# SBUF laid out with the large tensors first and the small columns last, in a fused attention-and-FFN block

## What is computed

```python
def attn(x):                       # x is layer-normalised already
    n = ln(x, g, b)
    W1, W2 = mlp(n, h1_w1, h1_b1, h1_w2, h1_b2), mlp(n, h2_w1, h2_b1, h2_w2, h2_b2)   # 128 -> 512 -> 128, gelu
    t = tril(W1 @ W2.T) @ n
    x1 = x + ln(gelu(t), g, b)
    return x + mlp(ln(x1, g, b), fm_w1, fm_b1, fm_w2, fm_b2)

def ffn(x):                        # ternary weights, each with a scale by output feature
    h = silu(x @ w1 * s1) * (x @ w2 * s2)          # 128 -> 512
    h = gelu(gelu(h @ a * sa) @ b * sb)            # 512 -> 512 -> 512
    return h @ w3 * s3                             # 512 -> 128

x = x + layernorm(attn(layernorm(x)))
x = x + layernorm(ffn(layernorm(x)))
```

## Time and profile before

| | |
|---|---|
| median of 3 runs | 364.95 us (364.9 to 365.11) |
| profiled execution, its own time | 365.25 us |
| its span, first to last instruction | 363.5 us |
| PE busy in the span | 351.9 us, 97%, 1786 matmuls |
| DVE, ACT, POOL busy | 319.9, 302.2, 153.2 us |
| mean granted TensorE clock | 0.995 |

### The profile page before, as it was taken

One profiled execution on the slowest core, in us unless ns is written; L12 is line 12 of the kernel. 1 busy time (PEld: TensorE's weight loads), 2 busy tenths in 40 slices (PEclk: granted clock), 3 DMA queues, 4 the chain that ended last, 5 costly groups with the idle time before them and its releaser, 6 DMA issues.

```text
span 363.5 us, 6043 instructions
## 1 busy us (share of the span) xinstructions
PE 351.9 (97%) x1786; PEld 290.1 (80%) x1786; DVE 319.9 (88%) x953; ACT 302.2 (83%) x546; POOL 153.2 (42%) x227
## 2 busy tenths in 40 slices
PE   6999999999999999999999999999999999999991
PEld 5886888788888888888888888888788878778990
DVE  5989999999999999899968999998878998958844
ACT  5999999996888979976789798889698489769890
POOL 3587868430581165109430276025450292053311
PEclk9999999999999999999999999999999999999998
DMA  7614300000000000000000000001010001000101
GB/s 231 174 58 148 114 4 1 0 3 0 3 0 0 2 9 23 0 0 2 1 29 3 0 2 2 0 0 32 1 31 0 0 2 31 0 2 0 32 30 32
DMA packets 8946, 9.08 MB, mean 25 GB/s; under 512 B 720, under 2 KB 6864, under 8 KB 8912
## 3 DMA queue, kind: packets, MB, share of 16 engines
q1 hardware_dynamic: 8368, 8.41, 7.7%
q10 hardware_dynamic: 544, 0.26, 0.3%
HBM read 6.57 MB, written 2.10 MB: 24 GB/s over the span
## 4 chain that ended last, share of the span: by engine, by line
PE 78%; ACT 10%; DVE 6%; issue 2%; DMA 1%; SPq 0%; POOLq 0%; POOL 0%; DVEq 0%; ACTq 0%
PE bank L1236 10%; PE bank L1234 10%; PE bank L1250 8%; PE bank L1251 8%; PE bank L1111 4%; PE bank L1115 4%; PE bank L1112 4%; PE bank L1130 4%; PE bank L1127 4%; PE bank L1128 4%; PE bank L1216 4%; PE bank L1219 4%; PE bank L1055 3%; ACT h_hidden_hi L511 3%; ACT bank L516 2%
## 5 line engine op out<-in xcount | busy, mean ns | idle before, releaser
L722 DVE TENSOR_TENSOR ffn_gate_lo<-bank,ffn_gate_hi 128x512 fp32r<-128x512 f32 (+1 forms) x72 | 43.9, 623 | 8.8 <-ACT bank L587 7.9
L511 ACT ACTIVATE h_hidden_hi<-bank,cols 128x512 fp32r<-128x512 f32 x64 | 43.7, 697 | 7.7 <-PE bank L1115 7.0
L587 ACT ACTIVATE bank<-bank,cols 128x512 f32<-128x512 f32 (+1 forms) x72 | 44.1, 640 | 0.7
L722 DVE TENSOR_TENSOR h_hidden_lo<-bank,h_hidden_hi 128x512 fp32r<-128x512 f32 x64 | 42.3, 677 | 0.4 <-ACT bank L516 0.2
L516 ACT ACTIVATE bank<-bank,cols 128x512 f32<-128x512 f32 x64 | 41.9, 670 | 0.3
L1234 PE MATMUL bank<-ffn_gate_hi,ffn_w_hi 128*128 128x512 f32 (+1 forms) x108 | 40.4, 379 | 0.0
L1236 PE MATMUL bank<-ffn_gate_lo,ffn_w_hi 128*128 128x512 f32 (+1 forms) x108 | 39.6, 373 | 0.0
L581 ACT ACTIVATE ffn_h_hi<-bank,cols 128x512 fp32r<-128x512 f32 (+1 forms) x36 | 23.2, 647 | 13.2 <-PE bank L1236 9.5
L369 POOL TENSOR_TENSOR XR<-X,ln_x_r 128x512 f32<-128x512 f32 x8 | 8.3, 1041 | 52.5 <-DVE bank L867 51.3
L581 ACT ACTIVATE ffn_gate_hi<-bank,cols 128x512 fp32r<-128x512 f32 (+1 forms) x36 | 23.7, 679 | 7.2 <-PE bank L1236 4.3
L1216 PE MATMUL bank<-yT_hi,ffn_w_hi 128*128 128x512 f32 (+1 forms) x72 | 27.0, 379 | 0.2 <-ACT raw L604 0.2
(11 more groups left out here) (162 smaller groups left out, 1118.9 us busy)
## 6 DMA issues: line engine op xcount, KB each, us to landing
raw<-ffn_w SPq DMA_DIRECT2D x5, 512.0 KB, 3.6
out<-X SPq DMA_DIRECT2D x7, 256.0 KB, 2.3
raw<-attn_w SPq DMA_DIRECT2D x6, 256.0 KB, 4.9
X<-x SPq DMA_DIRECT2D x3, 256.0 KB, 5.1
raw<-ffn_w SPq DMA_DIRECT2D x1, 256.0 KB, 3.1
X<-x SPq DMA_DIRECT2D x1, 128.0 KB, 2.4
X<-x ACTq DMA_DIRECT2D x1, 128.0 KB, 2.7
out<-X SPq DMA_DIRECT2D x1, 128.0 KB, 1.9
```

Source lines behind the costliest of these rows:

```text
L511: nc.scalar.activation(dst, bank(f"{L}u{j}", c)[:, :], ACT.Gelu, bias=bias_of(L, j)).then_inc(*hi[L].done(c, j))
L587: nc.scalar.activation(u, u, ACT.Gelu, scale=cols[:, C_HS[L] + j:C_HS[L] + j + 1]).then_inc(*act2[L].done(c, j))
L722: return nc.vector.tensor_tensor(dst, whole, high.bitcast(f32), ALU.subtract)
```

## The change

The small column tensors (cols, gate_half, gate_coef, fm_bias, fm_b2, neg_half, zeros, ones, lo_sums, lo_any, lo_flag, warm, quiet) are declared behind the large ones instead of between them, and warm and quiet become the two columns of one tensor, warm_quiet. bc, ident and mask keep their place in the list. No instruction is added, removed or reordered on any engine. Two read another name: the activation that warms up ACT's table (L457) writes column 0 of warm_quiet, and the eight memsets of POOL (L333) column 1.

```diff
--- before.py
+++ after.py
@@ -119,17 +119,9 @@
         X = sb("X", [P, TILES, D])
         Aw, Fw = halves("attn_w", [P, 6 * DI]), halves("ffn_w", [P, ffn_w.shape[1]])
         raw = sb("raw", [P, 6 * DI])
-        cols = sb("cols", [P, columns.shape[1]])
         bc = sb("bc", [P, 2, D])
-        gate_half, gate_coef = sb("gate_half", [P, J]), sb("gate_coef", [P, J])
-        fm_bias, fm_b2 = sb("fm_bias", [P, J]), sb("fm_b2", [P, 1])
         ident = sb("ident", [P, P])
         mask = sb("mask", [P, 2, P])
-        neg_half, zeros = sb("neg_half", [P, T]), sb("zeros", [P, T])
-        ones = sb("ones", [P, 1])
-        lo_sums, lo_any = sb("lo_sums", [P, FP]), sb("lo_any", [P, FP])
-        lo_flag = sb("lo_flag", [1, 1])
-        warm, quiet = sb("warm", [P, 1]), sb("quiet", [P, 1])
 
         NF, XR, XRB = sb("NF", [P, T, D]), sb("XR", [P, T, D]), sb("XRB", [P, T, D])
         n_tok = halves("n_tok", [P, T, D])
@@ -140,6 +132,15 @@
         SC = halves("sc", [P, SEQS, 3, P])
         HH, HM = halves("h_hidden", [P, HS, N]), halves("fm_hidden", [P, FS, N])
         HG, HF = halves("ffn_gate", [P, J, N]), halves("ffn_h1", [P, J, N])
+        cols = sb("cols", [P, columns.shape[1]])
+        gate_half, gate_coef = sb("gate_half", [P, J]), sb("gate_coef", [P, J])
+        fm_bias, fm_b2 = sb("fm_bias", [P, J]), sb("fm_b2", [P, 1])
+        neg_half, zeros = sb("neg_half", [P, T]), sb("zeros", [P, T])
+        ones = sb("ones", [P, 1])
+        lo_sums, lo_any = sb("lo_sums", [P, FP]), sb("lo_any", [P, FP])
+        lo_flag = sb("lo_flag", [1, 1])
+        warm_quiet = sb("warm_quiet", [P, 2])
+        warm, quiet = warm_quiet[:, 0:1], warm_quiet[:, 1:2]
 
 
         FN = raw[:, 0:N].rearrange("p (t d) -> p t d", t=T)
```

## The result

The changed kernel takes 361.61 us (median; 359.81 to 361.94 over 4 runs) against 364.96 us (364.9 to 365.11 over 4) for the kernel before: a ratio of 0.9898, interval 0.9864 to 0.9931. It is 1.0% faster, about 3.4 us. The profiled execution took 361.94 us.

What follows compares the result with a forecast made beforehand. PE was taken as the bound, 97% busy, so matmul count times pace sets the time. All terms summed to 0 on 365.25 us profiled, 0.3 above the median of the runs: forecast 364.9 us, range 361.3 to 368.0.

Steps and rivals of the forecast that it cites:

- the faster rival: Whole kernel: a gain over 0.7 us, chance 0.24, of which 0.22 by the matmul stream and 0.02 by drift.
- DMAs, ACT, DVE, POOL, weight loads: cost 0.: All readers and writers except PE's moving operand: new start addresses cost 0, with weight loads bounded by 0.4 us either way.
- PE's moving operand. This is the term that decides ... I take 0.: Matmul reads of the moving tensors, now at multiples of 64: taken as 0, a fixed-cost gain at most 1.5 us.
- a cost in proportion to the columns: PE's moving operand: a larger gain growing with matmul width, not excluded and without a row for its price, chance 0.05.
- The counts and the room for it.: PE: 1,192 matmuls of 512 columns and 272 narrower; for some 350 us each nanosecond goes straight into the span.
- 15.56 busy, hold slack: Last 23 us of the kernel: PE busy for 15.56 us, the only stretch said to hold slack.
- faster: the start address holds the matmul stream back: PE's moving reads lose time when starting 32 bytes off: 363.5 or 360.5 us; gain over 0.7 us, chance 0.22.
- least in the last stage: Sign of the faster rival: the whole timeline shrinks in proportion, with the smallest shrinkage in the last stage.
- slower: the two streams fall into step: PE's weight loads and moving operand both start at multiples of 64: 2 ns per matmul, 367.6 us, chance 0.12.
- if it grew with the columns: Slower rival's larger price: 4 ns on a 512-wide matmul, 5.1 us more, 370.0 us; chance 0.04.
- The estimate from the Trainium skill: PE at 512 columns: 215.7 ns against 17 ns more in the trace; if wholly the start address, 23 us less, some 342.

Runs made afterwards that it cites:

- m1: Computation left out, x copied and matmuls streamed at various operand starts: 512 columns took 226.7 ns at distance 0, 233.3 at 32 bytes.
- e2: Changed kernel with 32 unused bytes ahead of the weights, moving everything behind X, weights included: 361.88 us, ratio 0.9896 to the kernel before.
- e3: Kernel before the change with 32 unused bytes behind X, ahead of the weights: 365.06 us, ratio 0.9992.
- e6: Changed kernel with 128 unused bytes ahead of bc, so working tensors lie 128 bytes from the weights: 364.65 us, ratio 0.9989.
- m2: m1 with other offsets, 64-column weights and 384 columns: for 512 columns, 227.1 ns at 256 bytes, 229.4 at 320, 232.3 at 384.
- e7: Changed kernel with the last chunk's FFN slices shifted 32 bytes, so its 256-column layer matmuls have distance 32: 361.59 us, ratio 0.9909 to the kernel before.
- e8: e7 run again, beside a repeat of the changed kernel (361.96 us): 361.75 us, ratio 0.9918 to the kernel before.

## Why the prediction was wrong, step by step

The forecast was 364.9 us, no difference; 361.61 us was measured, 1.0% less and clear of the noise. That is inside the stated range (361.3 to 368.0), in the part that it held for the faster rival.

- **DMAs, ACT, DVE, POOL, weight loads: cost 0.** Right. Of the groups of the earlier trace rows all kept their means within 5 ns except n_tok_hi's copy, 17 ns slower (0.14 us of ACT in all), and ffn_w_lo, 6 ns slower. Both have the wrong sign for a gain, and neither is near 3.4 us.
- **"PE's moving operand. This is the term that decides ... I take 0."** This is the step that failed. That it decides was right, its value was wrong: −4.18 ns on each 512-wide matmul, −5.0 us, and +2.8 ns on the FFN's 256-wide ones, +0.5 us. Two arguments led to 0. The first was that the pace is in proportion to the columns (233 and 116), so that a fixed cost of the start can't exceed 1 ns. What it left open was a cost in proportion to the columns, at a chance of 0.05. The effect is neither: m1 at distance 0 has 226.7 and 119.6, at 32 it has 233.3 and 116.7, a loss of 6.6 ns at 512 columns and a gain of 2.9 at 256. The proportion was a property of that one distance. The second was that four other readers and writers don't mind their start. They don't, and it says nothing of PE, whose loads are busy for 80% of the span beside its matmuls, so that two of its operands are read at a time.
- **The counts and the room for it.** 1,192 and 272 matmuls, each nanosecond going straight into the span: nearly so. Of the 5.0 us that the 512-wide steps gave, 1.7 us came back in the longer steps, nearly all of it where PE is held up. The 3.3 us left, less 0.4 on narrower matmuls, are the 2.9 from the first matmul to the last. The reading of the last 23 us, "15.56 busy, hold slack", was loose: from 340 to 355 us PE is busy for 14.85 of 15 us, and most of the slack is the 7.5 us behind its last matmul.
- **Rival "faster: the start address holds the matmul stream back".** The side was right. The price was close (3.4 ns taken over from DVE rows, 360.5 us; 4.2 ns measured), but by luck, since the mechanism is not the one that it named. It took the moving operand's own start to matter. e2 is fast with every moving operand 32 off, e3 is slow with every one at a multiple of 64, e6 is slow with all at a multiple of 64. The sign it gave for the last stage ("least in the last stage", but a gain) was wrong too: the last stage's steps became slower.
- **Rival "slower: the two streams fall into step".** It had the mechanism, the distance between the two operands, and the sign for the width that it read it from: the scores' 120 ns against 116. Those were two steps, and all the 256-wide ones of scores and the product with n average 118.2; but with the bare stream's 119.6 in step, and the last stage's move from 116.8 to 119.6, that sign was right. It set that aside in part as the doing of the 128-wide neighbours. Where it went wrong is the step "if it grew with the columns": at 512 columns the effect has the other sign, −6.6 ns in m1. No 512-wide matmul of the trace before was in step, so the sign there couldn't be read; the range should have treated it as open.
- **The estimate from the Trainium skill.** The Trainium skill (TensorE: Matmul & The Clock Gate, "Wait — 56ns, not 53.3ns?") gives 215.7 ns for 512 columns, in a series of bf16 matmuls. m1 agrees with it for bf16, 215.8 ns. For fp32r the best was 226.7 ns, so of the 17 ns above that figure that the prediction puzzled over, some 6 were the distance (an estimate, 233 less 226.7) and some 11 come with the operand type (226.7 less 215.8).

What stays open: why the repeat is 256 bytes, why the sign turns between 256 and 512 columns, and whether the time is lost in the load of the weights or in the moving stream. The runs show paces, not what happens within a matmul. That a load takes part is supported by the exchange of offsets and by the change of weights' width moving the paces, but no run had a stream without loads. Nor does a run tell whether the distance that counts is to a matmul's own weights or to the next ones, which load while it streams: in m1 and m2, and among the 512-wide matmuls of the kernels, all weights start alike modulo 256.

## What to carry to other kernels

In a TensorE-bound fp32r kernel, treat the distance between the starts of moving operand and weights, modulo 256 bytes, as a free knob, worth 3% on the bare stream and 1% in this kernel: measure it on a bare stream of the kernel's own widths, then place one small pad. Weigh it by width, since 512 columns wanted 0 here and 256 columns wanted 32; in this kernel the 1,192 wide ones decide, and serving the narrow ones too gave no time (e7, e8). And where a trace holds only one setting of something, a neat proportion in it bounds nothing about the other setting; the few places that already have the other one (the earlier trace rows here) say more than the rows of all other engines, with the sign left open for other sizes.

## What the runs showed of the hardware that was not expected

- fp32r matmuls of 512 columns have a pace that depends on two start addresses together: 226.7 ns at distance 0 and 233.3 at 32 bytes, up to 236.7 at 4 bytes, with ACT, DVE and POOL idle. bf16 doesn't show it (215.8 to 216.0 ns at distances of 0, 16 and 32 bytes).
- The Trainium skill (TensorE: Matmul & The Clock Gate, "Step-by-step: what each phase is for") has it that loading the next weights takes no read bandwidth from the running matmul. For bf16 these paces give no reason to doubt it. For fp32r the pace moves with where the weights start (226.7 ns at distance 0, 233.3 with the weights alone 32 bytes past), which a fully independent load wouldn't explain. So the measurement speaks against it for fp32r, though no run here shows the stream without loads.
- The sign turns with the width: 119.6 against 116.7 ns at 256 columns, 226.7 against 233.3 at 512, under 1 ns apart at 384.
- The fast pattern is a state of the stream. After four transposes it took 4 to 11 steps (the first of 313 to 323 ns, the others of 224 to 237) until it was back, after four plain 128-wide fp32r matmuls three (the first of 283 or 284).
